# The second expert pass of a macaron block: picked tokens by indirect transfers instead of all tokens

## The reference, cut to what matters

```python
x = x + 0.5 * ffn(layernorm(x))      # first expert pass
x = x + attn(layernorm(x))           # linear attention, 16 heads of 32
x = x + 0.5 * ffn(layernorm(x))      # second expert pass

def ffn(x):
    logits = einsum('bsd,ed->bse', x, gate_w) + gate_b
    probs = softmax(logits, axis=-2)             # over the 1024 tokens
    vals, idx = top_k(probs over tokens, K)      # 8 tokens for each expert and batch
    merged = sum over k of vals * x[idx]         # one vector per batch and expert
    h = gelu([merged, 1] @ w1[e])                # 513 x 2048 for each expert
    o = [h, 1] @ w2[e]                           # 2049 x 512 for each expert
    out = zeros; out[idx] += o * vals            # a token can be picked by several experts
```

## Time and profile before

| | |
|---|---|
| median of 3 runs | 2545.33 us |
| the profiled execution, its own time | 2545.41 us |
| its span, first to last instruction | 2543.3 us |
| mean granted TensorE clock | 0.926 |
| PE / DVE / ACT / POOL busy | 83 / 34 / 30 / 22% |
| bytes moved | 770.23 MB, mean 303 GB/s |
| chain of waits | PE 47%, DMA 32%, DVE 7%, ACT 4%, POOL 4% |

### The profile page before, as it was taken

One profiled execution on the slowest core, in us unless ns is written; L12 is line 12 of the kernel. 1 busy time (PEld: TensorE's weight loads), 2 busy tenths in 40 slices (PEclk: granted clock), 3 DMA queues, 4 the chain that ended last, 5 costly groups with the idle time before them and its releaser, 6 DMA issues.

```text
span 2543.3 us, 44353 instructions
## 1 busy us (share of the span) xinstructions
PE 2106.8 (83%) x18828; PEld 1228.6 (48%) x18828; DVE 855.2 (34%) x1674; ACT 765.5 (30%) x1321; POOL 554.0 (22%) x645
## 2 busy tenths in 40 slices
PE   6979999999999999888888888888766655666565
PEld 3436666666656566566666666666511111111111
DVE  6831111111111112577777677777400000000006
ACT  6722111111111112466555656656400000000000
POOL 3210000000000000566666666656300000000000
PEclk9989999999999999899999999999888887788886
DMA  9759999999999997443333333333399999999998
GB/s 361 305 200 395 397 407 407 405 413 399 412 409 405 399 395 288 177 135 114 105 113 114 120 107 118 114 105 105 143 414 424 424 423 421 423 423 425 424 424 322
DMA packets 127459, 770.23 MB, mean 303 GB/s; under 512 B 11648, under 2 KB 11648, under 8 KB 74016
## 3 DMA queue, kind: packets, MB, share of 16 engines
q1 hardware_dynamic: 118048, 717.07, 71.9%
q10 hardware_dynamic: 9216, 50.34, 4.8%
HBM read 660.41 MB, written 100.66 MB: 299 GB/s over the span
## 4 chain that ended last, share of the span: by engine, by line
PE 47%; DMA 32%; DVE 7%; ACT 4%; POOL 4%; issue 3%; SPq 1%; POOLq 0%; DVEq 0%; ACTq 0%
PE ps L258 44%; DMA big<-in_L_ffn_w 30%; DVE big L266 2%; PE ps L262 2%; DVE big L1253 1%; SPq L18 1%; POOL s L1201 1%; DVE big L1173 1%; POOL s L1227 1%; DMA big<-in_L_attn_x 1%; POOL big L1210 1%; ACT big L1101 1%; DMA x_scratch<-big 1%; DVE big L1133 1%; DMA xt_scratch<-big 1%
## 5 line engine op out<-in xcount | busy, mean ns | idle before, releaser
L258 PE MATMUL ps<-big 128*32 128x512 f32 (+5 forms) x13896 | 1089.0, 434 | 313.7 <-DMA big<-in_L_ffn_w 227.9
L258 PEld LDWEIGHTS ps<-big 128*32 128x32 f32 (+2 forms) x13896 | 405.4, 129 | 916.6 <-issue 527.7
L266 DVE TENSOR_TENSOR big<-ps,big 128x512 f32<-128x512 f32 (+1 forms) x565 | 340.1, 649 | 141.4 <-PE ps L258 105.3
L258 PE MATMUL ps<-wth,xth 128*128 128x512 f32 x768 | 309.0, 402 | 3.0 <-ACT big L794 3.0
L258 PE MATMUL ps<-wth,xtl 128*128 128x512 f32 x768 | 299.6, 390 | 0.0
L258 PE MATMUL ps<-wtl,xth 128*128 128x512 f32 x768 | 299.0, 389 | 0.0
L677 ACT ACTIVATE big<-ps 128x512 f32<-128x512 f32 x64 | 38.2, 597 | 836.2 <-PE ps L258 836.2
L1198 POOL TENSOR_TENSOR big<-big 128x1 f32<-128x1 f32 x64 | 35.1, 549 | 929.1 <-ACT big L1051 878.5
L701 DVE COPY big<-ps 128x128 f32<-128x128 f32 x64 | 18.3, 286 | 638.3 <-PE ps L637 638.3
L258 PE MATMUL ps<-wo,s 128*128 128x512 f32 x768 | 213.5, 431 | 1.4 <-ACT s L1104 1.4
L803 DVE TENSOR_SCALAR big<-ps,big 128x512 f32<-128x512 f32 x64 | 48.1, 751 | 403.6 <-PE ps L258 403.6
(11 more groups left out here) (98 smaller groups left out, 1708.2 us busy)
## 6 DMA issues: line engine op xcount, KB each, us to landing
big<-in_L_ffn_w SPq DMA_DIRECT2D x256, 2048.0 KB, 17.6
p_scratch<-big ACTq DMA_DIRECT2D x64, 768.0 KB, 10.3
big<-p_scratch SPq DMA_DIRECT2D x64, 768.0 KB, 4.5
big<-in_L_attn_x SPq DMA_DIRECT2D x16, 1024.0 KB, 13.4
xt_scratch<-big SPq DMA_DIRECT2D x16, 1024.0 KB, 11.4
big<-xt_scratch SPq DMA_DIRECT2D x16, 1024.0 KB, 16.2
big<-in_L_attn_x SPq DMA_DIRECT2D x64, 256.0 KB, 2.9
x_scratch<-big SPq DMA_DIRECT2D x64, 256.0 KB, 3.2
```

Source lines behind the costliest of these rows:

```text
L258: return nc.tensor.matmul(o, l, r, start=start, stop=stop, skip_group_check=True)
L266: return nc.vector.tensor_tensor(o, p, q, op)
```

## The change

x2 is stored twice: to `out` (all tokens), and to a scratch tensor with rows of 544 floats, 512 of x2 and the token's 32 weights. Only tokens that some expert picked are then read back, finished and written over in `out`. FX is gone. In its place stand XS, sixteen tiles of 128 rows x 544: tile i = 8h + k holds, on partition 32q + e, the k-th token that belongs to expert e in batch 4h + q. A token belongs to the first expert that picked it, so each is handled once; unused places get an index beyond the tensor, which the indirect transfers skip.

```diff
+    XW = D + E
+    xmd = nc.dram_tensor("x2_weight_scratch", (B * S, XW), F).ap()
+    x2s = xmd.rearrange("(n p) d -> n p d", p=128)
...
+        XS = [at(wo_at + XW * i, XW) for i in range(11)] + [at(xs_at + XW * i, XW) for i in range(5)]
+        PICK, RANK = M[0][:, 0, :], M[0][:, 1, :]
+        WT = [BK[:, 32 * i:32 * i + 32] for i in range(16)]
...
-            return g % 4 if g < 4 * E else 4 + g % 4
+            return g % 4 if g < 4 * E else (4, 5, 6, 7, 2, 0, 1, 3)[g % 8]
...
+        def store_mt(sp, b):
+            sp.wait_ge(s_mt, 8 + b + 1)
+            sp.dma_start(xmd[S * b:S * b + S, D:XW].rearrange("(c p) e -> p c e", p=128), MT).then_inc(d_mt, 16)
...
-                    if (g + 4) // (4 * E) == p:
-                        load_chunk(sp, g + 4)
+                    ahead = 8 if p else 4
+                    if (g + ahead) // (4 * E) == p:
+                        load_chunk(sp, g + ahead)
...
-                if p == 1 and 8 <= e < 20 and e % 2 == 0:
-                    load_fx(sp, 8 + (e - 8) // 2)
-            if p == 1:
-                for i in (14, 15):
-                    sp.wait_ge(s_used, 8 * E - 3)
-                    load_fx(sp, i)
...
+                if p == 1 and 1 <= e < 3:
+                    rank_pe(pe, e - 1)
...
+                if p == 1 and 1 <= e < 3:
+                    rank_dve(dve, e - 1)
+                if p == 1 and e < 2:
+                    pick_dve(dve, e)
+                if p == 1 and e >= 16:
+                    weight_dve(dve, e - 16)
...
-                    sp.dma_start(x2s[n - 1], X2).then_inc(d_x2[(n - 1) % 2], 16)
+                    sp.dma_start(x2s[n - 1][:, 0:D], X2).then_inc(d_x2[(n - 1) % 2], 16)
+                    sp.dma_start(outs[n - 1], X2).then_inc(d_x2[(n - 1) % 2], 16)
+                if n >= 13 and (n - 13) % 8 == 0 and n < NT:
+                    store_mt(sp, (n - 13) // 8)
...
+            sp.wait_ge(s_av, NT)
+            sp.wait_ge(s_op, NT)
+            load_chunk(sp, 4 * E + 3)
+            load_chunk(sp, 4 * E + 4)
+            sp.wait_ge(s_x2, NT)
+            load_chunk(sp, 4 * E + 5)
+            sp.wait_ge(s_x2n, NT)
+            sp.wait_ge(d_x2[0], 32 * (NT // 2))
+            sp.wait_ge(d_x2[1], 32 * (NT // 2))
+            load_chunk(sp, 4 * E + 6)
+            sp.wait_ge(s_lg3, NT // 4)
+            sp.wait_ge(s_wt, 16)
+            load_chunk(sp, 4 * E + 7)
+            store_mt(sp, 7)
             sp.wait_ge(s_mg, 16)
             load_b2(sp)
+            sp.wait_ge(d_mt, 16 * B)
...
+        def rank_pool(pool):
+            pool.wait_ge(s_c, NT)
+            nc.gpsimd.iota(RANK, [[1, S]], base=1, channel_multiplier=0, ...)
...
+        def pick_dve(dve, h):
...
+            nc.vector.tensor_scalar(PICK, M[1][:, h, :], 0.0, None, ALU.not_equal).then_inc(s_own, 1)
+
+        def rank_pe(pe, h):
+            pe.wait_ge(s_rank, 14)
+            pe.wait_ge(s_own, 7 * h + 1)
+            for i in range(2):
+                t = mm(ps[:, 2 + i, :], EARLIER, PICK[:, 512 * i:512 * i + 512], True, True)
+            t.then_inc(s_cnt, 1)
+
+        def rank_dve(dve, h):
...
+            for i in range(2):
+                P_ = PICK[:, 512 * i:512 * i + 512]
+                nc.vector.scalar_tensor_tensor(out=P_, in0=ps[:, 2 + i, :], scalar=0.0, in1=P_, op0=ALU.is_equal,
+                                               op1=ALU.mult).then_inc(s_own, 1)
...
+            tt(PICK, PICK, RANK, ALU.mult).then_inc(s_own, 1)
...
+            nc.vector.max(T8, PICK).then_inc(s_own, 1)
...
+        def gather_pool(pool):
+            pool.wait_ge(d_mt, 16 * B)
+            for i in range(2):
+                pool.wait_ge(d_x2[i], 32 * (NT // 2))
+            pool.wait_ge(s_op, NT)
+            for i in range(16):
+                pool.wait_ge(s_own, 7 * (i // 8) + 7)
+                nc.gpsimd.indirect_dma_start(
+                    out=XS[i], out_offset=None, in_=xmd,
+                    in_offset=bass.IndirectOffsetOnAxis(ap=IDX[:, i:i + 1], axis=0),
+                    bounds_check=B * S - 1, oob_is_err=False).then_inc(d_pick[i // 8], 16)
+
+        def weight_dve(dve, i):
+            dve.wait_ge(d_pick[i // 8], 16 * 8)
+            nc.vector.transpose(WT[i], XS[i][:, D:XW]).then_inc(s_twt, 1)
 
         def final_pe(pe):
+            pe.wait_ge(s_twt, 16)
+            for i in range(16):
+                h = i // 8
+                pe.wait_ge(s_o, 3 + h)
+                pe.wait_ge(s_fout, i - 3)
+                for q in range(4):
+                    R_ = slice(32 * q, 32 * q + 32)
+                    t = mm(ps[R_, i % 4, :], WT[i][R_, :], O[R_, h, :], True, True)
                 t.then_inc(s_fin, 1)
 
         def final_dve(dve):
+            for i in range(16):
                 dve.wait_ge(s_fin, i + 1)
+                nc.vector.scalar_tensor_tensor(out=XS[i][:, 0:D], in0=ps[:, i % 4, :], scalar=0.5,
+                                               in1=XS[i][:, 0:D], op0=ALU.mult, op1=ALU.add).then_inc(s_fout, 1)
+
+        def final_pool(pool):
+            for i in range(16):
+                pool.wait_ge(s_fout, i + 1)
+                nc.gpsimd.indirect_dma_start(
+                    out=outr, out_offset=bass.IndirectOffsetOnAxis(ap=IDX[:, i:i + 1], axis=0),
+                    in_=XS[i][:, 0:D], in_offset=None,
+                    bounds_check=B * S - 1, oob_is_err=False).then_inc(d_fs, 16)
+            pool.wait_ge(d_fs, 16 * 16)
```

More of the change, by code:

```diff
@@ L172, in macaron_block @@
         SQ2 = [SM[:, 230 + i:231 + i] for i in range(2)]
+        ROW0 = [SM[:, 232 + h:233 + h] for h in range(2)]
+        NONE = SM[:, 240:248]
+        EARLIER = SM[:, 256:384]
+        IDX = nc.alloc_sbuf_tensor_at("idx", [128, 16], mybir.dt.uint32, offset=base + 4 * (sm_at + 160))[:, :]
         NG = NT // 4
@@ L179, in sems @@
             return [sem(f"{name}{i}") for i in range(n)]
-        d_gw, d_gb, d_bias, d_b1, d_b2 = (sem(n) for n in ("d_gw", "d_gb", "d_bias", "d_b1", "d_b2"))
+        d_gw, d_bias, d_b1, d_b2 = (sem(n) for n in ("d_gw", "d_bias", "d_b1", "d_b2"))
         d_xg, d_ring, d_wst = sems("d_xg", NX4), sems("d_ring", 8), sems("d_wst", 2)
@@ L185, in macaron_block @@
         d_x1, d_x2 = sems("d_x1", 4), sems("d_x2", 2)
-        d_fl, d_fs = sems("d_fl", 3), sem("d_fs")
+        d_mt, d_pick, d_fs = sem("d_mt"), sems("d_pick", 2), sem("d_fs")
+        s_rank, s_cnt, s_own, s_twt = (sem(n) for n in ("s_rank", "s_cnt", "s_own", "s_twt"))
         s_cst, s_selc, s_tri, s_gwT, s_gt, s_bk, s_ht0 = (sem(n) for n in (
@@ L364, in merge_transpose_act @@
             act.wait_ge(s_mtok, e)
+            if e > 8:
+                act.wait_ge(d_mt, 16 * (e - 8))
             nc.scalar.copy(MT, ps[:, k, 0:256].rearrange("p (c e) -> p c e", c=8)).then_inc(s_mt, 1)
@@ L1227, in attention_pool @@
                     nc.gpsimd.tensor_tensor(ATL, AT, ATH.bitcast(F), ALU.subtract).then_inc(s_atl, 1)
-        def final_sp(sp):
-            for i in range(NT // 4):
-                h, c = i // 8, i % 8
-                dst = outs[32 * h:32 * h + 32].rearrange("(r c) p d -> c p r d", r=4)[c]
-                sp.wait_ge(s_fout, 4 * i + 4)
-                sp.dma_start(dst, FX[i]).then_inc(d_fs, 16)
-            sp.wait_ge(d_fs, 16 * (NT // 4))
-        def final_pe(pe):
-            pe.wait_ge(s_o, 4)
-            for i in range(NT // 4):
-                h, c = i // 8, i % 8
-                pe.wait_ge(s_fout, 4 * i - 4)
-                for r in range(4):
-                    R_ = slice(32 * r, 32 * r + 32)
-                    t = mm(ps[:, 4 * (i % 2) + r, :], M[1][R_, h, 128 * c:128 * c + 128], O[R_, h, :], True, True)
+        def rank_pool(pool):
+            pool.wait_ge(s_c, NT)
+            nc.gpsimd.iota(RANK, [[1, S]], base=1, channel_multiplier=0,
+                           allow_small_or_imprecise_dtypes=True).then_inc(s_rank, 1)
+            pool.wait_ge(s_rank, 1)
+            nc.gpsimd.memset(EARLIER, 1.0).then_inc(s_rank, 1)
+            pool.wait_ge(s_rank, 2)
+            nc.gpsimd.affine_select(out=EARLIER, in_=EARLIER, compare_op=ALU.is_ge, fill=0.0, base=-1,
+                                    pattern=[[1, 128]], channel_multiplier=-1).then_inc(s_rank, 1)
+            for q in range(3):
+                pool.wait_ge(s_rank, 3 + q)
+                nc.gpsimd.memset(EARLIER[32 * q:32 * q + 32, 32 * q + 32:128], 0.0).then_inc(s_rank, 1)
+            for h in range(2):
+                for q in range(4):
+                    pool.wait_ge(s_rank, 6 + 4 * h + q)
+                    nc.gpsimd.memset(ROW0[h][32 * q:32 * q + 32, :], float(S * (4 * h + q) - 1)).then_inc(s_rank, 1)
@@ L1276, in _ @@
             hidden_pool(pool, 1)
+            rank_pool(pool)
+            gather_pool(pool)
+            final_pool(pool)
         @block.scalar
```

88 lines of the change are left out of this document (36 added, 52 removed).

## The result

The changed kernel took 2502.55 us (median of four runs, 2500.54 to 2505.4) against 2546.91 (four runs of the kernel before); the ratio is 0.9827 with a 95% interval of 0.9811 to 0.9843. Five more runs gave 2507.87 against 2549.71 on the same chip, 0.9846 (0.9823 to 0.9868). The forecast was 2501 us. I take the profiled execution of 2500.54 us apart, span 2498.8, against the one of before, 2545.41 us, span 2543.3.

What follows compares the result with a forecast made beforehand. Bytes were taken as both limits: 16.8 MB read back in the second expert pass and 16.8 MB written in the tail. 2545.4 - 37.8 (FX loads) + 10.2 (gather) + 5.5 (weight rows) + 1.0 (attention) - 23.4 (tail) = 2500.9 us; range 2486 to 2527.

Steps and rivals of the forecast that it cites:

- Stream: Second expert pass, to the last weights: FX loads gone -37.8 us, gather +10.2, weight-row stores +5.5; last chunk at 2465.0.
- The weight rows: Start of second pass: eighth store of 128 B pieces, then SP's wait for it, empties the queue; +5.5 us, bounds 1 and 10.
- The ring: Weight slots of the second pass: deeper prefetch itself worth nothing, since the DMA engines are already at 101%.
- Attention: Attention stage: 64 more stores mostly fit the slack before X2 is overwritten; +1 us, bounds 0 and 6.
- Ranks: Early second pass: VectorE's rank work, about 5.5 us per half, hidden by PE's slack and prefetch; 4 us if not.
- Tail: After the last weights: 7.2 us to start, sixteen scatters at 1.4, landing 3.2; 32.8 us against 56.2, so -23.4.
- (b): Tail: scatters run one after the other, through 1024 descriptor bytes or waiting for rows to land; no tail gain, 2527; chance 0.13.
- (a): Tail: descriptors are cheap, at or below 0.7 us per transfer, so VectorE paces the tail at 20.6; 2489; chance 0.12.
- t: Tail: POOL's price for one indirect transfer, taken as 1.4 us, between 0.4 and 3.2.
- (c): Attention: weight-row stores hold up load_p or X2's stores beyond 6 us slack; +20 us, 2520; chance 0.06.
- (d): Tail: POOL's descriptors cost so much that the kernel is slower, from 4.2 us per transfer; 2558 at 5 us; chance 0.07.
- (e): Gather and scatter: rows of repeated picks aren't skipped, 230 rows more both ways, 1 MB, +2.6 us; 2504; chance 0.03.

Runs made afterwards that it cites:

- third store: The changed kernel with each x2 tile stored once more in attention, to a scratch tensor (16.8 MB more); X2's tiles 12.15 us apart, as before the change.
- scatter_after: The changed kernel with 2496 bytes for software descriptors and POOL waiting for all sixteen finishing steps before its first scatter; tail 44.8 us.
- best: The changed kernel with 2304 bytes for software descriptors and without SP's wait for d_mt before the second pass; 2504.84 us, ratio 0.9818.
- twice_mt: The changed kernel with each store of the weight rows issued a second time, to another scratch tensor; stream 643.0 us, 0.8 more.

## Why the prediction was right, point by point

- **The sum.** Forecast 2500.9, profiled 2500.54, median 2502.55. That it came so near is luck: the stream gained 1.7 us more than forecast, attention 1.6 more, the tail 3.3 less, and 0.4 less lie around the span. The signs that it gave are there for the most part: experts at 19.7 us, the last weights at 2462.7, a hole of some 3 us, scatters 1.29 us apart, a DMA share of 0.33 in the tail. The first scatter is late.
- **Stream.** Predicted 22.1 us less, measured 23.8. The gather was priced at 10.2 and costs 9.6. The weight rows with SP's wait were priced at 5.5 and cost about 4: 3.0 for the wait, at most 1 for the small pieces, which I had put at 3. Adding both back, the removed FX loads are worth about 37 us; predicted 37.8.
- **The ring.** "The deeper prefetch itself is worth nothing" is the sentence that was wrong. The sum had it right, since it let chunks 132 to 135 take FX's place, but that is exactly what the depth does, and it is worth 12 us (654.4 against 642.2).
- **Attention.** Predicted +1 us. The first wait for X2's store grew from 5.9 to 7.0 us, nothing else shows, and the stage's end lies within what executions differ by.
- **Ranks.** Hidden, as predicted: two passes of 1.23 us each per half and the others, with no gap in the stream from 1860 on.
- **Tail.** Predicted 32.8 us, measured 36.1. The distance of the scatters was put at 1.4 and is 1.29 (15 of them, -1.6 us). The first scatter starts 9.6 us after the last weights instead of 7.2: the last expert's matmuls ran at a lower clock (3.29 instead of 1.97 us), and 0.9 us pass between VectorE's first end and POOL's record. (In other executions of the same code it is 8.2 and 12.6 us.) The last scatter and its landing took 3.2 instead of 4.6. The missing term is the pauses, 3.9 us in all: I had named the 1024 bytes of L1316 only as a reason for a wholly serial tail, rival (b), and not as a pause after every seventh transfer. The matmuls and VectorE's steps were put down as hidden, and that was wrong as well: without the pauses POOL waits for late steps instead, and the time from the first scatter to the end stays at 26.0 to 27.3 us against 26.5.
- **Rivals.** (a) falls: t is 0.99 of work and 0.30 between. (b) falls as a whole and holds in the small. The fixed 2.0 us that the Trainium skill (DMA: Bandwidth & Descriptors, Anatomy of one DMA) gives each transfer from POOL comes to 2.6 us with the bytes of one scatter (an estimate by that section's formula); the trace has 2.2 us from the end of POOL's last record to the end of the span and 3.2 from its start, so the size is about right. It isn't paid in turn. (c) falls by the third store. (d) falls by t. (e) falls by the count of bytes. (Its 2.6 us took the rows both ways, though by the tail's own sum the bytes of the scatter are hidden; 1.3 would have been its price.)

## What to carry to other kernels

In a stage bound by bytes, count the bytes, and then look at the seams: what the queue holds at the moment at which the removed transfers used to run decides whether the saving is kept, and here half of what the stream gained hung on four more chunks of prefetch. A transfer of 128 rows by index costs POOL 1.3 us and little else, so a tail that writes 22% of the rows is worth it. Too little room for descriptors costs (from the first scatter to the end 32.2 us with 512 bytes, 26.5 with 1024), but room for the whole burst gave at most 0.5 us more here, because another wait, VectorE's late steps, stood right behind. A pause that can be seen is worth only what the next wait leaves of it. A wait that guards nothing on its own queue (SP's for d_mt) costs all that stands behind it, here 3 us.

## What the runs showed of the hardware that was not expected

- The room for software descriptors bounds the transfers under way: with 512, 1024, 2048 and 2304 bytes POOL made 3, 7, 14 and 15 scatters of 128 rows before it paused, and with 2496 bytes all sixteen (scatter_after). This fits nine places of 16 bytes per transfer and one place left free. Beside the stream the numbers vary a little (7, 8 and 1 gathers with 1024 bytes). A pause is 2.2 to 2.4 us with idle DMA engines and 17.2 us beside a saturated queue; in both it ends about 1 us after the last packet of the latest transfer. With 2048 bytes a pause among the gathers ended earlier than that.
- While POOL's scatters follow closely on one another, TensorE's completion signals come up to 4.9 us late (6.8 in best) and then in a burst, whoever waits for them. In the changed kernel the seventh signal, during POOL's fourth scatter, is the first that is late by more than 0.3 us. With all scatters after the last signal, none is late; beside rows of gathers none of the recorded ones is late by more than 1.0 us.
- SP stood 9.88 us in issuing one store of 1024 pieces with the queue full (twice_mt), against 0.37 for the one just before it.
